# Adding q by TensorE for half of the groups of a message pass, and filling q two groups ahead

## The reference

```python
h = node_features @ enc_W + enc_b
for l in range(N_LAYERS):
    cat = jnp.concatenate([h[src], h[dst], edge_features], axis=-1)
    m = jax.nn.relu(cat @ msg_W1[l] + msg_b1[l]) @ msg_W2[l] + msg_b2[l]
    agg = jax.ops.segment_sum(m, dst, num_segments=n_nodes)
    h = _gru_cell(agg, h, gru_Wih[l], gru_Whh[l], gru_bih[l], gru_bhh[l])
```

## Time and profile before

| | |
|---|---|
| median of 3 runs | 2399.44 us (2396.63 to 2401.02) |
| the profiled execution | 2401.86 us, its span 2400.0 us |
| PE busy over the span | 1915.8 us (80%) |
| DVE busy | 1800.5 us (75%) |
| POOL busy | 1649.4 us (69%) |
| ACT busy | 1100.1 us (46%) |
| q additions at L1353 | 156 instructions, 108.1 us |
| PSUM additions at L1355 | 156 instructions, 107.1 us |
| edge products at L1873 | 1248 instructions, 63.2 us |

### The profile page before, as it was taken

How to read it: one execution, slowest core, us unless ns; L and a number is a source line. 1 busy time by engine, 2 the same in 40 slices (tenths; PEclk the granted TensorE clock), 3 DMA queues, 4 the chain that set the end, 5 groups by cost and what they waited for, 6 DMA issues and landing times. The chain is left out here.

```text
span 2400.0 us, 48319 instructions
## 1 busy us (share of the span) xinstructions
PE 1915.8 (80%) x15773; PEld 1552.5 (65%) x15773; DVE 1800.5 (75%) x6473; ACT 1100.1 (46%) x2756; POOL 1649.4 (69%) x1641
## 2 busy tenths in 40 slices
PE   4999468998599997489896689984889994699951
PEld 3878337887358876258775268774368883578841
DVE  8999644887248999559999559999437776367775
ACT  1445223344124444334443324442548885478873
POOL 5777645777657777577777577775567775777764
PEclk9999757999699999699998889997879996699985
DMA  7999915997238999358998269996157774267751
GB/s 225 335 318 350 297 34 191 349 361 237 58 106 270 304 303 301 93 155 284 304 303 277 74 200 300 302 304 218 28 118 222 227 223 150 37 214 228 218 158 41
DMA packets 308195, 522.94 MB, mean 218 GB/s; under 512 B 105947, under 2 KB 141349, under 8 KB 307748
## 3 DMA queue, kind: packets, MB, share of 16 engines
q1 hardware_dynamic: 236256, 437.07, 53.7%
q0 software_dynamic: 52160, 52.25, 10.6%
q10 hardware_dynamic: 19588, 31.50, 3.8%
HBM read 353.76 MB, written 166.87 MB: 217 GB/s over the span
## 5 line engine op out<-in xcount | busy, mean ns | idle before, releaser
L1845 PE MATMUL ps<-big 128*128 128x256 f16 (+1 forms) x13038 | 1526.5, 277 | 87.0 <-DMA big<-kept 61.3
L1845 PEld LDWEIGHTS ps<-big 128*128 128x128 fp8e5 x13038 | 1281.8, 99 | 298.6 <-issue 105.8
L742 POOL DMA_INDIRECT ringG<-tab,src_i x1137 | 1133.0, 997 | 391.1 <-issue 325.2
L1273 DVE SCALAR_TENSOR_TENSOR ringG<-ringG,same 128x64 f32<-128x64 f32 x2075 | 578.3, 279 | 52.4 <-DMA ringG<-tab,src_i 17.3
L843 ACT ACTIVATE ringG<-big 128x512 uint8<-128x512 uint8 (+1 forms) x684 | 367.3, 624 | 4.3
L1273 DVE SCALAR_TENSOR_TENSOR edge_side<-edge_side,same 128x64 f32<-128x64 f32 x1245 | 344.1, 276 | 1.5
L873 ACT ACTIVATE ringG<-ringG 128x512 f32<-128x512 f32 x156 | 97.7, 627 | 443.8 <-DVE ringG L1355 443.8
L1395 DVE SCALAR_TENSOR_TENSOR ringG<-ringG,expo 128x65 f32<-128x65 f32 x830 | 237.9, 287 | 78.6 <-ACT ringG L884 9.1
L742 POOL DMA_INDIRECT ringG<-in_x,src_i x188 | 201.2, 1070 | 94.6 <-issue 52.9
L1246 DVE COPY_PREDICATED ringG<-twins,ringG 128x256 uint32<-128x256 int32 (+3 forms) x532 | 196.6, 370 | 70.2 <-ACT ringG L843 69.7
L831 ACT ACTIVATE big<-ps 128x512 int32<-128x512 f32 (+1 forms) x228 | 125.4, 588 | 262.4 <-PE ps L1845 262.0
(11 more groups left out here) (274 smaller groups left out, 1432.5 us busy)
## 6 DMA issues: line engine op xcount, KB each, us to landing
big<-kept SPq DMA_DIRECT2D x156, 768.0 KB
sums<-ringG SPq DMA_DIRECT2D x260, 256.0 KB
edge_side<-ef_mix SPq DMA_DIRECT2D x156, 256.0 KB
edge_side<-q_at_start SPq DMA_DIRECT2D x156, 256.0 KB
big<-kept SPq DMA_DIRECT2D x78, 480.0 KB
big<-kept SPq DMA_DIRECT2D x78, 384.0 KB
sums_w<-ringG SPq DMA_DIRECT2D x104, 264.0 KB
kept<-big SPq DMA_DIRECT2D x26, 768.0 KB, 8.8
```

Of the source, the lines that this page charges most:

```text
L742: return pool.indirect_dma_start(out=out_ap, out_offset=None, in_=table, in_offset=bass.IndirectOffsetOnAxis(ap=index, axis=0))
L1273: return v.scalar_tensor_tensor(now, before if u == 0 else source[:, (u - 1) * D:u * D], same[:, c:c + 1], now, ALU.mult, ALU.add)
L1845: mm = pe.matmul(ps[:, bank_of(k, i, m), 0:2 * n] if wide else to, hot[t][:, u * P:(u + 1) * P], opener[:, 0:2 * n] if wide else split[:, ...
```

## The change

For groups whose number modulo four is 1 or 3, VectorE no longer adds q. TensorE opens the group's PSUM bank with the product of the identity and the tile of q (float32, 128 x 512), and the eight edge products accumulate onto it, so that the addition at L1355 brings in both. TensorE therefore waits for `q_filled` ahead of these groups' products. VectorE's fill runs two groups ahead and not one: two groups are filled before the loop, and iteration g fills group g + 2. The rings, the loads and the other engines' loops are as before.

```diff
-QAHEAD = 1
+QAHEAD = 2
+PE_ADDS = (1, 3)
...
-                    v.wait_ge(q_filled, l * NG + g + 1)
-                    link(v.tensor_tensor(rows, rows, ringQ[:, g % QRING], ALU.add))
+                    if g % GROUPS not in PE_ADDS:
+                        v.wait_ge(q_filled, l * NG + g + 1)
+                        link(v.tensor_tensor(rows, rows, ringQ[:, g % QRING], ALU.add))
...
-            def edge_products(l, s, bank, loaded, added):
+            def edge_products(l, s, bank, loaded, started, added):
...
+                if started is not None:
+                    pe.wait_ge(q_filled, started)
                 settle()
+                if started is not None:
+                    pe.matmul(ps[:, EBANK + bank, :], ident[:], ringQ[:, s, :], start=True, stop=False)
                 for u in range(COLS):
                     mm = pe.matmul(ps[:, EBANK + bank, u * D:(u + 1) * D], ringE[:, s, u * P:(u + 1) * P],
-                                   w_e_mix[:, l * D:(l + 1) * D], start=True, stop=True)
+                                   w_e_mix[:, l * D:(l + 1) * D], start=started is None,
+                                   stop=started is None or u == COLS - 1)
...
+                                  l * NG + g + 1 if g % GROUPS in PE_ADDS else None,
...
+                                          at(GROUPS, l * NG + q + 2 - GROUPS) if (q + 1) % GROUPS in PE_ADDS else None,
```

## The result

Before: 2399.05 us, the median of 20 runs (2393.62 to 2403.64). After: 2403.34 us, the median of 20 (2399.24 to 2408.51). The ratio is 1.0019, 95% interval 1.0013 to 1.0025: 4.3 us more, where 2 less were forecast. The profiled execution of after took 2401.25 us, 2.1 under its median, with a span of 2399.4.

What follows compares the result with a forecast made beforehand. VectorE was taken to set the pace before, a closed loop of waits through TensorE and VectorE after; +6 (loop trips), +4 (first trips) and -13 (last trips) made -3 us, 2397 us for the median, range 2377 to 2420.

Steps and rivals of the forecast that it cites:

- the whole saving: Rival: VectorE keeps the pace at 18.6 us a trip and all 57 us come out, 2342 us; chance 3 in 100.
- The identity product: On TensorE, two a trip: each 128 x 512 float32 product takes 0.96 us, range 0.9 to 1.06.
- The hand-over from VectorE: From the end of VectorE's fill to TensorE's identity product: estimated 0.1 us, up to 0.3 more in the range.
- The loop: TensorE's products, ScalarE's spreads, VectorE's mend and fill wait in a circle: 20.3 us a trip against 20.05, +6 us; chance 52.
- the first trips: First trip of each pass, two identity products late: +1.9 us in the third pass, +1.0 in the first, +4 in all.
- VectorE's own trip: VectorE's work per trip without two additions: 18.6 us, fitting inside the 20.3 with 1.7 us idle at the mend.
- The last three trips: Short units at each pass's end, TensorE out of the way: 4.4 us a pass come out, -13 us.
- A load that loses its lead: q, needed an iteration sooner, arrives 4.7 to 6.9 us after S (start of a group's first big addition); loss hidden in slack.
- Slower: q comes late: Rival at the fill's first step: q's lateness exceeds VectorE's slack, 21.1 us a trip, +19 us, 2418 us; chance 15.
- TensorE's own work as the pace: Rival: no wait binds, TensorE's work sets 19.57 us a trip, -22 us in all, 2377 us; chance 15.

Runs made afterwards that it cites:

- e8_late_early: The changed kernel with q asked for one step sooner and both mends of an iteration after the eighth fill step; ratio to before 0.9907, 2376.89 us.
- e3_early_q: The changed kernel, with SyncE asking for q one step sooner, ahead of the store it used to follow; ratio to before 0.9959.
- e7_cheap_early: The changed kernel with q asked for one step sooner and the identity product replaced by a same-shape bf16 product on other data; ratio to before 0.9893, 2372.04 us.
- f3_loop_mend_early: The changed kernel with q asked for one step sooner and only the mends of each trip's first group after the eighth fill step; ratio 0.9934, 2386.20 us.
- f2_fill2_early: The changed kernel without identity products (VectorE adds q for all groups, fill two ahead), q asked for one step sooner; ratio to before 0.9977.
- e2_adds_only: The changed kernel with TensorE's additions kept but q filled only one group ahead, as before; ratio to before 1.1002, 2647.18 us.

## Why the prediction was wrong

**That the whole saving would not come: right.** VectorE gave back 78 additions and a pass hardly moved. After Perfetto Trace Analysis, "Identifying the Most-Contended Engine", of the Trainium skill, one would have judged TensorE by its rate of arithmetic and its weight loads, the latter 15.74 us of 20 in before; in e8_late_early it is the bound with 16.53 of weight loads and 20.00 of products. The trip back to back in the earlier trace rows was the better witness.

**The identity product: right in kind, 0.1 too long.** 0.96 us was taken from other float32 products; it is 780.52 - 779.66 = 0.86, and 0.94 where the fill had just ended. The hand-over from VectorE was 767.78 - 767.64 = 0.14, not 0.1.

**The loop: right.** 20.18 us against 20.28. The nine trips of three passes at the loop's own pace cost +3.8 us (e3_early_q), forecast +6; the first trips +2.8, forecast +4. e7_cheap_early shows the products in the loop, f3_loop_mend_early the mend that closes it. VectorE's own trip was put too short: 18.83 us where it waits for nothing (e7_cheap_early), not 18.6. So it had 1.25 us to spare at the mend (e3_early_q) and not 1.7.

**The last three trips: right in kind, if q is in time.** Forecast -13. With early q they give -14.9, of which 2.8 come with the fill two ahead (f2_fill2_early) and the other 12 with the additions. In the changed kernel they give -7.5.

**The failed step is "A load that loses its lead".** Its arithmetic put q at 4.7 to 6.9 us after S, needed after 5.1 or 5.8, and closed with "VectorE loses 0.7 us a trip, inside the 1.7 to spare". Three things were wrong with that.
- The middle of the range stood for all loads, and the range ended too soon. They scatter: 5.9 us after S at 950.73, but 8.2 at 956.71. Of the 45 loads that VectorE waited for, twelve came later than 6.9. What comes late in one trip is not returned by the next: none of the nine trips of a pass is shorter than the loop's 20.18. Most of the waits are where the step said they would be, in the odd group after the short iteration (29 of 45, 20.9 of 33.7 us).
- The slack, 1.25 us and not 1.7, exists only while the loop binds. In the last three trips, from which the whole gain was to come, there is none. Late q took 172.1 - 164.7 = 7.4 us there, and 548.9 - 545.4 = 3.6 in the nine trips; the first trips were 1.4 shorter than with early q.
- The same load was priced in a rival (2418, 15 in 100) and at nothing in the forecast, as if it came either late everywhere or nowhere.

With q in time each term of the sum is within 2.2 us of the forecast: e3_early_q lies 8.3 us below before in the passes, against -3. Late q, put at nothing, adds 9.6 there, which makes about +1.3 between the passes of before and after. So that 2403 lies near 2397 is partly luck: the other terms together came out 5.3 us better than forecast. The rival "Slower: q comes late" had the right resource, and with +19 us was 15 too high.

The rule of the Trainium skill weighed there (DMA: Bandwidth & Descriptors, "Anatomy of one DMA"; an estimate of 2.6 us for 256 KB, for a DMA from GpSimd's queue) would have q never late. The traces disagree: 7.2 us from issue to use at 949.55, with the DMA engines at a share of 0.90. Going by the rows was right; taking their middle was not.

**TensorE's own work as the pace** (2377, 15 in 100) is what one gets after two more edits, e8_late_early: nine trips -13.2, where 27 x -0.48 = -13 had been forecast. That its 2376.89 us meets the 2377 so closely is chance, for first and last trips came out otherwise (-1.4 and -10.7, against +4 and -13).

## What to carry to other kernels

When a change asks for data one step earlier, follow the load: compare its whole scatter, not its middle, with the new need, and do so in every stage, for slack that hides it in the steady loop may be missing in the trips that bring the gain. Work that moves to an engine with time to spare still adds its full length to any loop of waits that runs through it; find the wait that closes the loop (here one mend between fill steps) and move that. Two costs that partly hide each other give more together than one by one: late mends took off 6 us, early q 14, both 27.

## What the runs showed of the hardware

TensorE's granted clock fell in some of its longer waits, which made them dearer. In the changed kernel's last trips TensorE waited 3.03 us for ScalarE, and from 947 to 952.5 us the granted clock was 0.50, the level of 1.2 GHz; the identity product of 0.86 us then took 1.71 (950.84 to 952.55):

```profile
947.05 0.59 PE L1847 MATMUL ps<-opener,big 128*128 128x512 f16 x1 [3.03 <-ACT big L832]
...
950.84 1.92 PE L1877 MATMUL ps<-edge_side,ident 128*128 128x512 f32 x2
952.55 0.60 PE L1879 MATMUL ps<-w_e_mix,edge_side 128*128 128x64 bf16 x8
```

Two stretches of that kernel, ahead of the wait and behind it:

```profile
940.00:943.50 3.50, 3.50 (x34) 2.67 (x33) 3.46 (x15) 0.63 (x1) 2.86 (x3) 1.00 0.93 286
947.00:952.50 5.50, 5.45 (x18) 2.97 (x19) 4.67 (x20) 4.93 (x11) 4.52 (x4) 0.50 0.90 273
```

In e2_adds_only this happened in each steady trip, after the wait of 5.71 us:

```profile
842.50:844.50 2.00, 2.00 (x6) 0.78 (x7) 0.03 (x1) 0.00 (x0) 1.59 (x2) 0.50 0.71 200
```

So a loop of waits through TensorE can lengthen itself: 2.1 of the 27.3 us of such a trip. Not every wait did this: behind a wait of 2.88 us in f3_loop_mend_early, at 1631.37, the granted clock was 1.00. What made the difference was not followed up.
